# Two steps of a quantised decoder layer on one core: where GpSimd adds a residual, and where VectorE takes one batch's statistics

## The reference, cut to what matters

```python
x = x + attn(layernorm(x))                       # int4 quantised attention
x = x + xattn(layernorm(x), fside, ctx)          # the stage of the change
x = x + ffn(layernorm(x))                        # top-2 routed, 8 experts' slots, shared weights

def smooth_quant_linear(x, w):                   # x [T, D], w [O, D]
    s = sqrt(max(amax_x_by_column, 1e-6) / max(amax_w_by_column, 1e-6))
    xs, ws = x / s, w * s
    x_scale = amax(|xs|, rows) / 127;  w_scale = amax(|ws|, rows) / 127
    return round(xs / x_scale) @ round(ws / w_scale).T * x_scale * w_scale.T

h = smooth_quant_linear(xe, fside[b]); gate, up = split(h)
out = smooth_quant_linear(silu(gate) * up, ctx[b])
```

## Time and profile before

| | us |
|---|---|
| median of 3 runs (lowest, highest) | 924.59 (924.5, 926.39) |
| the profiled execution's own time | 926.92 |
| its span, first to last instruction | 925.0 |
| PE busy | 733.8 (79%) |
| DVE (VectorE) busy | 727.6 (79%) |
| ACT (ScalarE) busy | 597.5 (65%) |
| POOL (GpSimd) busy | 198.4 (21%) |
| mean granted TensorE clock | 0.893 of full |

### The profile page before, as it was taken

How to read it: one execution, slowest core, us unless ns; L and a number is a source line. 1 busy time by engine, 2 the same in 40 slices (tenths; PEclk the granted TensorE clock), 3 DMA queues, 4 the chain that set the end, 5 groups by cost and what they waited for, 6 DMA issues and landing times. The chain is left out here.

```text
span 925.0 us, 15582 instructions
## 1 busy us (share of the span) xinstructions
PE 733.8 (79%) x5141; PEld 309.0 (33%) x5141; DVE 727.6 (79%) x1039; ACT 597.5 (65%) x1059; POOL 198.4 (21%) x271
## 2 busy tenths in 40 slices
PE   1567899999999999999974915565567279999997
PEld 0522232222222222222221214344345134444443
DVE  7899678999999999999999987888988854521111
ACT  4769545989889898989967416675557629651000
POOL 1110654002211111222120323214513220000010
PEclk9869998999999999999995857777868579999999
DMA  8600574222222222222123001110009520000000
GB/s 317 228 1 0 194 256 162 56 68 66 66 64 72 61 63 74 73 62 65 41 63 117 0 1 45 47 46 0 13 29 362 182 65 1 1 1 11 23 23 35
DMA packets 51596, 70.61 MB, mean 76 GB/s; under 512 B 13108, under 2 KB 27476, under 8 KB 51040
## 3 DMA queue, kind: packets, MB, share of 16 engines
q1 hardware_dynamic: 50272, 65.84, 22.3%
q0 software_dynamic: 1280, 4.20, 1.4%
HBM read 46.17 MB, written 19.12 MB: 71 GB/s over the span
## 5 line engine op out<-in xcount | busy, mean ns | idle before, releaser
L992 DVE TENSOR_REDUCE SWV<-PS 128x2 f32<-128x1024 f32 x256 | 300.6, 1214 | 14.8 <-PE PS L1447 13.6
L1881 ACT ACTIVATE slab<-PS 128x512 f32<-128x512 f32 x512 | 275.6, 595 | 34.5 <-PE PS L1580 26.6
L1563 PE MATMUL PS<-slab,HB 128*32 128x256 f32 x2048 | 163.6, 392 | 10.4 <-ACT HB L1865 10.4
L1580 PE MATMUL PS<-slab 50*128 50x512 f16 x512 | 124.4, 383 | 2.8 <-ACT slab L1881 0.3
L1447 PE MATMUL PS<-slab 48*128 48x512 f16 x512 | 100.7, 390 | 2.6 <-ACT slab L1837 1.3
L1754 PE MATMUL PS<-slab 128*128 128x512 f16 x384 | 86.0, 387 | 1.7 <-DVE slab L1336 1.4
L1765 PE MATMUL PS<-slab 128*128 128x512 f16 x384 | 83.0, 379 | 0.0
L1563 PEld LDWEIGHTS PS<-slab,HB 128*32 128x32 f32 x2048 | 41.7, 108 | 90.0 <-issue 64.0
L1368 DVE SCALAR_TENSOR_TENSOR WOT<-PS,cmax,WOT 128x512 f32<-128x512 f32 x8 | 6.0, 750 | 69.8 <-PE PS L1765 69.8
L1447 PEld LDWEIGHTS PS<-slab 48*128 48x128 f16 x512 | 24.6, 92 | 102.8 <-issue 94.5
L1362 DVE SCALAR_TENSOR_TENSOR slab<-HB,cmax,slab 128x512 f16<-128x512 f32 x32 | 23.8, 750 | 43.6 <-ACT slab L1983 43.6
(11 more groups left out here) (311 smaller groups left out, 1187.7 us busy)
## 6 DMA issues: line engine op xcount, KB each, us to landing
slab<-in_L_ffn_w SPq DMA_DIRECT2D x2, 4096.0 KB, 14.1
q_split<-slab SPq DMA_DIRECT2D x24, 256.0 KB, 2.7
k_split<-slab SPq DMA_DIRECT2D x24, 256.0 KB, 2.7
slab<-q_split SPq DMA_DIRECT2D x64, 96.0 KB, 2.6
slab<-k_split SPq DMA_DIRECT2D x64, 96.0 KB, 2.6
slab<-in_x SPq DMA_DIRECT2D x4, 1024.0 KB, 12.1
slab<-HB SPq DMA_DIRECT2D x128, 32.0 KB
slab<-in_fside_BxS2xS SPq DMA_DIRECT2D x4, 1024.0 KB, 5.3
```

The source lines that it names most:

```text
L992: nc.vector.tensor_reduce(NM[:, ring].rearrange("p (a x) -> p a x", a=2)[:, :, x], PS[:, bank:bank + 2, :], AX.X, ALU.max, negate=True).th ...
L1563: ins = nc.tensor.matmul(PS[32 * h:32 * h + 32, 6, cols], VST[:, r % 2, k, h, :], PROB[:, k, h, cols], start=k == half == 0, stop=k == KB ...
L1580: nc.tensor.matmul(PS[:, st_bank(2 * s + a), :], KP[rows, r, p, P * k:P * k + P], QP[rows, r, p, :], start=True, stop=True).then_inc(st_re ...
L1881: nc.scalar.activation(PROB[:, k, 2 * a + p], PS[:, st_bank(t), :], ACT.Exp, scale=score_scale).then_inc(probs, 1)
```

## The change

Two edits. `added(n)`, GpSimd's residual add, waits for `l_scale` (raised by L1150, the last instruction of `steps_of_rounding`) and no longer for `l_xs` (raised by L1139 in the same step). The statistics of batch 3, with the wait for GpSimd's first residual adds, move from the end of VectorE's step 0 to the place between `smooth(0)` and `steps_of_rounding(0)`.

```diff
                 b = batch(n)
                 pool.wait_ge(l_h, 4 * n + 4)
-                pool.wait_ge(l_xs, n + 3)
+                pool.wait_ge(l_scale, n + 3)
                 nc.gpsimd.tensor_tensor(X[:, 4 * b:4 * b + 4], X[:, 4 * b:4 * b + 4], LH[chain(n)], ALU.add
                                         ).then_inc(x2_done, 1)
...
             def meanwhile(n):
 
-                if n == 0:
-                    other_half_done(2 * KB)
-                    statistics(3 * KB, 4 * KB)
                 if n == 1:
...
                 smooth(n)
                 if n:
                     product(n - 1)
+                else:
+                    other_half_done(2 * KB)
+                    statistics(3 * KB, 4 * KB)
                 steps_of_rounding(n)
```

## The result

The changed kernel takes 928.64 us (median of 15 runs, 925.4 to 932.24), the kernel before 925.35 in its 15 runs (923.85 to 926.85). The ratio is 1.0041, 95% interval 1.003 to 1.0051: slower by 3.8 us by the ratio and 3.3 by the medians, where 2.6 was forecast. The execution that was profiled is one of the changed kernel's fastest (925.81, span 923.8), so its span is no measure; I read it by stretches between marks inside the second sublayer. R is the end of `steps_of_rounding` (L1150) as in the prediction.

What follows compares the result with a forecast made beforehand. VectorE was taken to bound the stretch holding both edits, up to the weights' load; 1.5 (step 4) + 2.1 (step 5) - 1.0 (statistics) = +2.6 us on the median 924.59 gave 927.2, range 924.9 to 930.0.

Steps and rivals of the forecast that it cites:

- Edit 1: Steps 0 and 1: batch 3's statistics fill VectorE's idle time before L1148, L1139 starts earlier; gain 1.0 us (0.6 to 1.3).
- Who comes first: Behind R in steps 4 and 5: VectorE's instruction starts first, GpSimd's add gets in at R + 1.01, before the next.
- the burst: Rival, step 4: VectorE's maxima keep GpSimd's add out until near R + 2.9; sum +1.4, 926.0 us; chance 0.12.
- GpSimd first: Rival, steps 4 and 5: the add gets in ahead of L1099 and L1166; sum +5.1, 929.7 us; chance 0.09.
- no exclusion: Rival, steps 4 and 5: maxima and GpSimd's add run together, nothing held; -3.1, 921.5 us; chance 0.11.
- Step 4: L1100 waits for GpSimd's add, L1122 starts at R + 7.22; +3.34 less 1.81 for L1149's freed hold: +1.5 us.
- Step 5: L1099 behind L1114 waits for GpSimd's add, L1122 starts at R + 6.43; +2.39 less 0.30: +2.1 us.
- L1149's own hold: L1149 waits for GpSimd's add at its old place; the edit removes 1.81 us in step 4, 0.30 in step 5.
- from step 6 on nothing gives it back: From step 6 to 690.45 VectorE is the chain, so the +2.6 us sum reaches the end unchanged.
- The 14.28 of the load follow: After VectorE's chain ends at 690.45, the load of the next sublayer's weights follows, taking 14.28 us.
- the clock: Not in the prediction; e1, the changed kernel rerun, named it: lock and clock, +3.5 to +4.5 us with wide scatter.
- the third hold: Not summed in the prediction; L786 held under GpSimd's L685 of step 6; e5 expected -0.9 to -1.2 us without it.

Runs made afterwards that it cites:

- e2: Kernel before with only the statistics of batch 3 moved, GpSimd's adds at their old place: ratio 0.9987 to the kernel before, -1.2 us.
- e6: As e5, with column maxima behind R in steps 4 and 5 by one-SBUF-input reductions in place of two-input pairs: ratio 0.9988 to the kernel before.
- e7: As e5, with half of each second-layer GpSimd residual add left out (two of four tiles, output not the reference's): ratio 0.9984 to the kernel before.
- e5: Changed kernel with the moments of batches 0 and 2 (L784, L786) moved from step 5 to behind L1142 of step 6: ratio 1.0021 to the kernel before.
- e9: e4 plus statistics of batches 0 and 2 in VectorE's gaps, their moments between L1148 and L1149 of step 7: ratio 0.9953 to the kernel before, 921.07 us.
- e3: Kernel before with only GpSimd's adds made to wait on l_scale, behind L1150: ratio 1.0042 to the kernel before, +3.9 us.
- e4: Batch 3 statistics moved as in the changed kernel; each GpSimd add halved, at the old place and behind next step's both_roots: ratio 0.9978 to the kernel before.

## Why the prediction was right

The sign, the mechanism and its place were right, and 928.64 lies in the range; the size was short by about 1.2 us, and +3.8 lies outside the +1.7 to +3.4 that the prediction gave as the ends of its sum (+3.3, by the medians, just inside).

- *Edit 1.* 1.0 forecast, 1.05 in the trace, 1.2 timed alone (e2). No collision with GpSimd.
- *Who comes first.* L1099 first, the add in at its end, L1100 behind it, as rows 6 had it. The add ran 5.32 and 5.34 (5.4 forecast). Of the rivals, the burst and GpSimd first are refuted by these rows, no exclusion by them and by e6 and e7.
- *Step 4.* L1122 at R + 7.22 forecast, 7.00 and 7.23 seen. The 0.2 between the two is TensorE's L1630: 0.84 in one profile, 1.11 in the other.
- *Step 5.* R + 6.43 forecast, 6.41 and 6.42 seen.
- *L1149's own hold, the gain of the edit*, was mis-sized as a constant. I took 1.81 from one execution; e2's profile, with GpSimd's add at the same place, had 1.10. Where it is smaller the edit costs 0.7 more.
- *The step that failed* is "from step 6 on nothing gives it back": I looked only for slack that would return time, not for a collision that a late VectorE would run into, and put that term at nothing. Measured from R of step 5, ScalarE and GpSimd hardly notice that VectorE is late: ScalarE's copies (L1946) end at R + 9.98 before and R + 9.97 after, and L685, which waits for the copy that ScalarE makes next (L1904), starts at R + 10.32 and R + 10.66. VectorE, 2.4 later, reaches L786 at R + 11.98 in place of R + 9.61, and so behind the start of L685 and no longer ahead of it. That is 0.9 to 1.2; with the moments moved (e5) the trace has 0.75 to 1.07 less.
- *"The 14.28 of the load follow"* took one execution's landing for a constant. It was 15.74 in e5's profile, of its slowest run (931.61), and 15.58 in e9's; where the load landed sooner, as in the changed kernel's profile, VectorE's path of 13.90 stood in the chain. By these figures it moves single runs by up to 1.8 us.

The terms as measured: -1.05 for edit 1; -1.1 to -1.8 and +3.1 to +3.3 in step 4; -0.3 and +2.4 in step 5; +0.9 to +1.2 in step 6. Taken together +3.3 to +4.5, where the timing has +2.8 to +4.7.

Rows 6 and the Trainium skill (SBUF — State Buffer, Who interferes with whom) differed on whether L611 shuts out a VectorE instruction with two SBUF inputs for its whole length. e9's rows agree with rows 6: L1176 starts 0.15 into L611 and takes its 2.24. For GpSimd's adds (L671, L692) the page's lock held in the traces read here.

What stays open: the changed kernel's runs scatter over 7 us and e5's over as much, those of the kernel before over 3 to 4. In the changed kernel's 15 runs the scatter goes with the mean granted clock: its two fastest (925.4, 925.81) had 0.897, its three slowest (931.09 to 932.24) 0.885 to 0.888, and the mean was 0.890, against 0.894 in 23 runs of the kernel before. So the clock is a rival for the missing 1.2 us. e5 speaks for the third hold (its mean clock was 0.891, about the changed kernel's, and its ratio lower), but its interval overlaps with the changed kernel's, and how the 1.2 divides between the two stays open. Whether a lower clock was the cause of the slow runs or went along with something else wasn't shown. TensorE's 3.09 of idle time ahead of L1630 doesn't bring it about by itself: e3 has it too, at 0.893 and with the narrow scatter.

## What to carry to other kernels

Before an instruction of GpSimd is moved, list what VectorE runs in the new place by its number of SBUF inputs: beside reductions, statistics and instructions with a PSUM operand GpSimd's adds were free, beside two SBUF inputs or a tiny TENSOR_SCALAR the second one waited to the end of the first, up to 4.2 us for 0.7 of work. (GpSimd's L611, with 8 elements a partition, held nothing up.) The old place had cost 1.4 to 2.1; the better cure here was shorter adds in free stretches (e4), not a later start. And when one engine is delayed but not its neighbours, check what these now do earlier in relation to it.

## What the runs showed of the hardware

- A blocked instruction got in 0.1 before the recorded end of the other, in both directions (VectorE's L1149, L1070 and L1100 before the end of an add, the add before the end of L1099), and GpSimd, waiting, got in ahead of a VectorE instruction that had still to wait for the one before it on its own engine.
- A reduction over tiles, 2048 elements with a stride (e6's L1117), took 3.71, a contiguous one of as many (L1142) 2.29.
- TensorE's 16 matmuls of one step (128x512 bf16, L1682 of step 2) took 5.31 in some profiles and 3.63 in others, of the same instructions in the same place. The windows over them (busy us of PE, PEld, DVE, ACT, POOL, then the granted clock), first of the kernel before, then of the changed one:

```profile
594.20:599.40 5.20, 5.20 (x16) 1.85 (x16) 2.27 (x4) 1.99 (x2) 3.95 (x2) 0.67 0.00 2
```

```profile
590.80:594.30 3.50, 3.50 (x16) 1.43 (x16) 2.25 (x3) 1.96 (x2) 3.26 (x2) 1.00 0.01 2
```

  Granted the full 2.4 GHz, TensorE is 1.7 us sooner than at a mean of 0.67 of it (some of the stretch at 1.2 GHz), on the chain of a step where no instruction was changed: more than edit 1 gains. So a single profiled span can't tell a change of 1 us: the changed kernel's span was 1.2 shorter than that of the kernel before, and it is the slower kernel.
